# Products of constants on TensorE in the heads and tails of the attention stages, and a shorter entry and exit, in a four-level transformer kernel

## What is computed

```python
x = x + 0.5 * _L0_ffn_ref(_layernorm(x, axis=-1), ...)   # 8 experts, top 2
x = x + _L0_attn_ref(_layernorm(x, axis=-1), ...)        # 16 heads, softmax
x = x + 0.5 * _L0_ffn_ref(_layernorm(x, axis=-1), ...)
x = x + 0.5 * _L1_ffn_ref(_layernorm(x, axis=-1), theta, phi, theta_noise, phi_noise)
x = x + _L1_attn_ref(_layernorm(x, axis=-1), ...)        # a state that decays from token to token
x = x + 0.5 * _L1_ffn_ref(_layernorm(x, axis=-1), theta, phi, theta_noise, phi_noise)
...
# level 2: a stack of 6 windowed attention and ffn layers, attention, the stack again
# level 3: 8 experts top 2 (gated), attention with rotary angles and exp scores, 8 experts again
```

## Time and profile before

| what | us |
|---|---|
| three runs: lowest, median, highest | 5185.12, 5185.85, 5190.96 |
| the profiled execution | 5185.4 |
| its span in the trace (1.8 us lie outside it) | 5183.6 |
| entry: until the first load of stage 0 | 0 to 12.2 |
| angles in the entry: ten DVE operations | 4.21 to 7.78 |
| angles in the entry: ACT's table load, sine | 1.28, 0.42 |
| stage 0, experts of level 0 | 12.2 to 273 |
| ACT's idle time before L559 at 51.09 and in the next such place, 66.49 | 3.75, 3.71 |
| stage 1, attention of level 0 | 273 to 463 |
| one first_score (L927) at clock 0.50, at 1.00 | 1.67, 0.94 |
| stage 4, decaying attention of level 1 | 748 to 914 |
| stage 7, attention of level 2 | 2664 to 2887 |
| turn_negmax (L939) to turn_negmax in it, from the second on | 21.6 |
| one exponential of ACT in it | 1.02 |
| stage 10, attention of level 3 | 4797 to 4993 |
| last DVE operation, last DMA, end | 5176.94, 5178.12, 5183.6 |

### The profile page before, as it was taken

One profiled execution on the slowest core, in us unless ns is written; L12 is line 12 of the kernel. 1 busy time (PEld: TensorE's weight loads), 2 busy tenths in 40 slices (PEclk: granted clock), 3 DMA queues, 4 the chain that ended last, 5 costly groups with the idle time before them and its releaser, 6 DMA issues. The chain is left out here.

```text
span 5183.6 us, 141391 instructions
## 1 busy us (share of the span) xinstructions
PE 4899.3 (95%) x49076; PEld 3434.4 (66%) x49076; DVE 3885.8 (75%) x7068; ACT 3436.2 (66%) x5889; POOL 2889.7 (56%) x3477
## 2 busy tenths in 40 slices
PE   8989978699999999999979699999999999989899
PEld 5666656377777777777656377777777777656656
DVE  3274347589999999999856499999999999855655
ACT  3344333488888888888856378888888888852642
POOL 0010015588888888888720488888888888710200
PEclk9998988799999999999979799999999999989999
DMA  1000000112111112111100112121211111110000
GB/s 45 1 6 35 1 8 3 44 42 61 49 51 51 53 53 57 47 54 50 45 16 1 41 45 57 47 55 49 57 53 51 51 53 53 43 38 1 8 25 9
DMA packets 110453, 195.58 MB, mean 38 GB/s; under 512 B 21408, under 2 KB 28848, under 8 KB 110256
## 3 DMA queue, kind: packets, MB, share of 16 engines
q1 hardware_dynamic: 110256, 192.89, 13.3%
HBM read 53.36 MB, written 1.05 MB: 10 GB/s over the span
## 5 line engine op out<-in xcount | busy, mean ns | idle before, releaser
L3222 POOL TENSOR_TENSOR stage_qk<-stage_halves 128x1024 f32<-128x1024 f32 x384 | 908.7, 2366 | 16.6 <-DVE stage_halves L3380 1.6
L3258 POOL TENSOR_TENSOR stage_qk<-stage_qk,stage_rnorm 128x1024 f32<-128x1024 f32 x384 | 731.2, 1904 | 8.0
L3251 POOL TENSOR_TENSOR stage_probs<-stage_probs,stage_rsum 128x768 f32<-128x768 f32 x384 | 565.6, 1473 | 257.8 <-DVE stage_rsum L3409 257.8
L2973 ACT ACTIVATE stage_probsT<-stage_flip 96x512 f32<-96x512 f32 x768 | 452.8, 590 | 221.4 <-PE stage_flip L2610 220.8
L3377 DVE TENSOR_TENSOR stage_halves<-stage_wide,stage_tables 128x1024 f32<-128x1024 f32 x384 | 469.3, 1222 | 144.5 <-ACT stage_square L2927 98.0
L3380 DVE TENSOR_TENSOR stage_halves<-stage_wide,stage_tables 128x512 f32<-128x512 f32 x768 | 490.6, 680 | 0.0
L2927 ACT ACTIVATE stage_square<-stage_wide 128x1024 f32<-128x1024 f32 x384 | 393.5, 1025 | 141.1 <-PE stage_wide L2558 136.7
L3389 DVE TENSOR_REDUCE stage_norm<-stage_square 128x16 f32<-128x1024 f32 x384 | 463.7, 1208 | 29.1 <-issue 29.0
L2575 PE MATMUL stage_turn<-ident,stage_qk 128*128 128x128 f32 x3072 | 478.9, 279 | 6.5 <-ACT stage_qkT L2947 6.5
L2610 PE MATMUL stage_flip<-ident,stage_probs 128*96 128x128 f32 x3072 | 469.6, 275 | 8.1 <-POOL stage_probs L3251 6.9
L2624 PE MATMUL stage_pv<-stage_probsT,stage_v_win 96*64 96x64 f32 x12288 | 464.7, 226 | 2.6 <-ACT stage_ctxT L2980 1.5
(11 more groups left out here) (304 smaller groups left out, 9984.3 us busy)
## 6 DMA issues: line engine op xcount, KB each, us to landing
stage_v_win<-stage_v SPq DMA_DIRECT2D x384, 192.0 KB, 2.5
stage_v_win<-stage_v SPq DMA_DIRECT2D x384, 128.0 KB, 2.4
stage_v_win<-stage_v SPq DMA_DIRECT2D x192, 64.0 KB, 2.2
stage_wq<-in_T_wq SPq DMA_DIRECT2D x12, 512.0 KB, 4.2
stage_wk<-in_T_wk SPq DMA_DIRECT2D x12, 512.0 KB, 4.8
stage_wv<-in_T_wv SPq DMA_DIRECT2D x12, 512.0 KB, 3.4
stage_wo<-in_T_wo SPq DMA_DIRECT2D x12, 512.0 KB, 3.4
stage_w_up<-in_L_w_up SPq DMA_DIRECT2D x8, 512.0 KB, 6.6
```

The lines of the kernel that those rows point to most:

```text
L2973: nc.scalar.activation(probsT[:, n % 2].rearrange("p h t q -> p (h t) q"), tiles4(flip)[0:REACH], ACT.Copy)\
L3222: nc.gpsimd.tensor_tensor(qk[:, n, :], halves[:, n % 2, 0, :], halves[:, n % 2, 1, :], ALU.add)\
L3251: nc.gpsimd.tensor_tensor(probs[:, m % 2], probs[:, m % 2], rsum[:, m % 2].to_broadcast([P, 2, 2 * HALVES, REACH]), ALU.mult)\
L3258: nc.gpsimd.tensor_tensor(heads, heads, rnorm[:, n, :].rearrange("p (h o) -> p h o", o=1).to_broadcast([P, LH, LD]), ALU.mult).then_inc(at ...
```

## The change

Four parts.

**Entry.** The signals are raised by POOL, DVE, ACT and PE, a quarter each, and POOL sets `minus_half` first. SP loads the first two pieces of x and `ident` (signal `entered`, for which it waits) and then the other six pieces of x (signal `rest`). The work on the angles moves into the class `Angles` and stage 0: its four loads are issued after the experts' loads, DVE's chain stands after `statistics(1)` and ahead of `base(0)`, ACT's sine after `copy_xT(1)`.

```diff
+            if angles:
+                angles.load(sp)
+            if out is not None:
+                rows = out.rearrange("b (h p) d -> p (b h) d", p=P)
+                for step in range(steps):
+                    sp.wait_ge(*sig("x", step, 1))
+                    sp.dma_start(rows[:, step * T:(step + 1) * T, :], chip.x[:, step * T:(step + 1) * T, :]).then_inc(loaded["left"], 16)
+                sp.wait_ge(*loaded("left", 1))
...
                     if e == 3:
                         ahead(step, copy_xT)
+                        if angles and step == 0:
+                            angles.sines(act)
...
             route(0, chain)
+            if angles:
+                dve.wait_ge(*loaded("rest", 1))
             ahead(0, statistics)
+            if angles:
+                angles.reduce(dve)
```

```diff
+            def fill(count):
+                for n in range(count):
+                    nc.tensor.matmul(quad[:, n % GROUPS, 0:P], chip.ident[:, :], chip.ident[:, :], start=True, stop=True, skip_group_check=True)
+
+            def warm(count):
+                for n in range(count):
+                    nc.tensor.matmul(duo[:, n % 2, 0:P], chip.ident[:, :], chip.ident[:, :], start=True, stop=True, skip_group_check=True)
...
                 ins.then_inc(sig["negmaxT"], 1)
+                if step == B - 1:
+                    fill(6)
...
                 ins.then_inc(sig["scores"], 1)
+                if softmax and step == B - 1:
+                    fill(1)
...
                     if runs(s):
                         bank_free(("probs", s, 6))
                         score(s, 6)
+                    elif s == -2:
+                        warm(1)
...
+            warm(6)
             for s in range(-3, B + 3):
                 body(s)
```

```diff
                 ins.then_inc(sig["ynT_psum"], 1)
-                fill(FILL_Y)
+                if step < B - 1:
+                    fill(FILL_Y)
...
                     weigh(s - 3)
+                elif 1 <= s < 3:
+                    fill(5)
...
                     project_td(s - 1)
+                elif s == B + 1:
+                    fill_wide(1)
...
                     project_gv(s - 1)
+                elif s == B + 1:
+                    fill_wide(2)
...
                     project_kr(s - 1)
+                elif s == B + 1:
+                    fill_wide(3)
...
                     project_w(s - 1)
+                elif s == B + 1:
+                    fill_wide(1)
...
                     output(s - 4)
+                elif 1 <= s < 4:
+                    fill(2)
...
                     project_miu(s)
+                elif B + 1 <= s < B + 3:
+                    fill_wide(4 * (s - B))
...
                     turn_y(s - 3)
+                elif s < 3:
+                    fill(6)
```

253 lines of the change are left out of this document (202 added, 51 removed).

## The result

The changed kernel took 5160.03 us in the median of five runs (5149.42 to 5164.99), the kernel before 5185.85. The ratio is 0.9945, with a 95% interval from 0.9931 to 0.9959: 25.8 us less, clear of the 0.2% that can be told. The profiled execution took 5160.11, its span is 5158.3. The forecast was 5158, with a range from 5143 to 5177. The sum is right within 2 us, but several of its terms are off by 4 to 9 us and cancel, so that closeness is luck; most of this part is about that.

The account below looks back on a forecast made before the run. TensorE was taken to run at its upper clock except in short stretches where stages begin or end, 143 us of them at 1.2 GHz in the four touched stages. The terms sum to -27.7 us from 5185.85, giving 5158, range 5143 to 5177.

Parts of the forecast that it names:

- Start: Kernel entry: four engines share raising the signals, so stage 0 begins near 5.7 instead of 12.2: -6.5 us.
- Angles: Stage 0: the angles' work on DVE and ACT fits into idle gaps: 0; 3.0 us if the cover were gone.
- output: Kernel exit: three quarters leave before the last x is done, SP waits only for the last 256 KB: -3.2 us.
- Price of a product: Added products on PE: 0.46 us each at the low clock, 0.29 at the high one, free where PE waits anyhow.
- Decaying stage: Stage 4: products lift the clock; head -5 us (-8 to +4), tail -3 us (-5 to +2).
- First attention: Stage 1: products lift the clock; head -1 us (-4 to +2.5), tail -2.5 us (-4.4 to +4).
- Third attention: Stage 7: products lift the clock; head -3 us (-9 to +3.5), tail -4 us (-9 to +5).
- Fourth attention: Stage 10, head: seventeen products in one row ahead of the second turn nearly offset the clock's gain: +0.5 us (-3 to +6).
- Stages in between: Stages other than the four with added products, ends aside: no change, 0.
- A: Rival: the clock gives nothing net, only start and end count, -9.7 us, 5176; chance 0.12.
- C: Rival: the clock comes up nearly at once everywhere, -50.9 us, 5135; chance 0.13.
- B: Rival: products are paid at the low clock ahead of real work, +31.8 us, 5218; chance 0.04.

Follow-up runs that it names:

- e5_no_rwkv: The changed kernel with the decaying stage as in the kernel before (4 and 6 products, on the weights): 5178.73 us, ratio 0.9982.
- e1_ends: The changed kernel with its new start and exit, but all products of constants as in the kernel before: 5176.69 us, ratio 0.9978.
- e3_again: The changed kernel measured again without any edit, for a second profile: 5164.20 us, ratio 0.9955.
- e4_no_l3: The changed kernel without the 26 products at the head of stage 10 (attention of level 3): 5154.96 us, ratio 0.9946.
- e6_table: The changed kernel with one added exponential on ACT in the entry, so that its table is loaded there: 5158.94 us, ratio 0.9954.
- e9_all: The changed kernel with the early table load, products among the first scores of stages 1 and 7, 13 in stage 7's waits and 6 stand-ins: 5162.16 us.
- e11_l0_scores: The changed kernel with two more products ahead of each of the first five scores of step 0 in stage 1: 5171.68 us, ratio 0.9962.
- e12_burst: The changed kernel with 16 products in a row ahead of step 2's projection in stages 1 and 7: 5171.88 us, ratio 0.9969.

## Why the prediction was right, and where it was not

**Start, -6.5.** 6.07 came. The step of this term that failed is the one on ACT's tables: it was noted that a load at the start goes away, and not that the load left over would stand behind PE's first result. It costs 1.28 us, so the start is worth 4.8.

**Angles, 0, and output, -3.2.** Both as worked out: DVE had 2.61 us left and ACT 2.05, and 3.2 us went at the exit. Of the sum's 9.7 for the ends, the trace has 8.0; the run with them alone has 10.0, with a scatter of 12 us.

**Price of a product.** 0.46 low holds. The 0.29 at the high clock was too much, as it came from a short row of four; rows of fifteen and seventeen take 3.62 and 3.96 us. PE in the changed kernel, around the long rows:

```profile
754.42 3.62 PE L1957 MATMUL stage_inner<-ident 128*128 128x128 f32 x30
757.97 0.65 PE L1994 MATMUL stage_turn<-stage_mixd,stage_pack 128*64 128x256 f32 x2
...
884.02 1.95 PE L1962 MATMUL stage_wide<-ident 128*128 128x128 f32 x16
887.44 0.41 PE L2063 MATMUL stage_turn<-ident,stage_yn 128*128 128x128 f32 x2 [1.47 <-DVE stage_yn L2448]
889.06 0.78 PE L2071 MATMUL stage_turn<-stage_pack,stage_gated 128*128 128x128 f32 x4 [1.21 <-DVE stage_gated L2456]
...
4788.38 3.96 PE L973 MATMUL stage_duo<-ident 128*128 128x128 f32 x34
```

With two instructions for each product, these rows are 15, 8 and 17 products: 0.24, 0.24 and 0.23 each. The seventeen ahead of the second turn of stage 10 delay it from 11.6 to 13.1 us after the stage's start, 1.5 where 2.7 was forecast, and the third turn is already 0.5 us earlier than before. The last turn_y of stage 4 waits 1.47 us for DVE behind its eight products, so they were covered, as the term had it.

**Decaying stage, -8.** Right mechanism, both terms too small. project_td follows the fifteen products at once and comes 1.1 us earlier in the stage than before, where it waited 1.76 us for POOL. The second project_td is 0.3 us later than before, so up to there the products cost what they gave; the third is 4.6 us ahead and the fourth 6.8, which is where the low stretch of 782 to 795 and a short one behind it are gone. By the fifth of the eight turns of y the stage is still 6.8 us ahead (term: -5), and the tail gives 7.0 more (term: -3). The tail's term left out the clock's fall at 873.7, which the windows of the earlier trace rows did not cover. Some 3 to 5 of the 13.8 us may not be the products', as the two kernels without the new ones (e5_no_rwkv, e1_ends) took 160.5 and 162.4 in one trace each, where the kernel before took 165.5.

**First attention, -3.5.** -5.7 in this trace, but +2.5 to +5.4 in four of nine. Over the nine the stage takes 188.3 us in the mean, 1.7 less than before.

**Third attention, -7.** This is the term of the sum that failed. It held in two of six traces (-8.3), and in four the stage lost 2.1 to 2.8. Of its two parts, the tail (-4) came out at -5.2 in the first trace. The head (-3, from -9 to +3.5) did not: the first turn of the maxima is 2.8 us earlier, but the second is 4.2 us later and the fourth 7.3 us later than before. In two of the others (e3_again, e4_no_l3) the head gained its 2.8 us, and it was the tail that failed: its last turn of the maxima came 5.4 us later after the one before than it used to. What the sum lacked in both is a fall of the clock at a place where it had stayed up before; both terms only counted low stretches that were there already. For the head it comes behind the last product. PE's timeline of the changed kernel:

```profile
2664.06 0.71 PE L973 MATMUL stage_duo<-ident 128*128 128x128 f32 x4
2666.54 1.15 PE L963 MATMUL stage_quad<-stage_k_heads,stage_q_heads 32*128 32x256 f32 x16 [1.76 <-DVE stage_negmax L1722]
2667.61 1.02 PE L937 MATMUL stage_turn<-stage_pack,stage_xT 128*128 128x128 f32 x4
2670.43 0.69 PE L980 MATMUL stage_turn<-ident,stage_negmax 128*128 128x128 f32 x2 [1.79 <-DVE stage_v L1683]
2671.04 2.09 PE L963 MATMUL stage_quad<-stage_k_heads,stage_q_heads 32*128 32x256 f32 x16
```

The last two products end at 2664.8. Then PE waits 1.76 us, does a narrow score, waits 1.79, and the score at 2671.04 takes 2.09 us instead of 1.15. The clock fell behind the products, and it stayed down for 44 us: the second turn of the maxima came at 62.9 us instead of 58.7. The fall alone does not make the bad course. In the two good traces (e5_no_rwkv, e6_table) the clock falls at the same place, 25.9 us after the stage's start against 25.7 here, but is back at 46.4 us instead of 70.1. Among the operations that ran meanwhile are scores, but also turns, projections and `weigh`, so why it stayed down is not shown. The prediction had put the head's worst case at +3.5 us and taken it for the case in which products don't raise the clock. In fact they do, and a fall comes after them.

**Fourth attention, +0.5.** -3.8 in seven of eleven traces with these products, -2.6 in one, and +0.9, +3.4 and +4.1 in the others. The clock was up in one piece from 4788 to 4930. 2.8 of the 3.8 us were won behind the last turn of x, where no product stands and which no term counted. A low stretch there became shorter, from 10 to 3 us. Windows before and after:

```profile
4949.00:4959.00 10.00, 9.37 (x62) 5.86 (x66) 2.99 (x5) 4.08 (x4) 0.00 (x0) 0.51 0.01 2
4931.00:4934.00 3.00, 3.00 (x25) 2.08 (x24) 1.01 (x1) 0.81 (x1) 0.00 (x0) 0.50 0.00 0
```

**Stages in between, 0.** Stages 0 (less its table load), 2, 3, 5, 6, 8 and 9 together took 3.9 us more. They scatter by 1 to 5 us between traces of the same code, so this is no effect of the change that could be shown.

**Rivals and the total.** The sum came out since stages 4 and 10 gave 10 us more than forecast and stage 7 and the table 10 less. That is luck. Of the rivals, A (no net gain of the clock) is what the products of stages 7 and 10 come to over many executions: without either group the kernel took 5159.5 and 5155.0. C was the closest in stage 4 alone (counted its way from the earlier trace rows, that stage gains about 11 us; 13.8 were measured). B, products paid at the low clock in the way of real work, was small in the changed kernel's first trace (among the new ones in the tails, two products of stage 7, inside 2849 to 2855); it showed more in the runs that added some (e9_all, e11_l0_scores, e12_burst).

The best supported account is this. Of the 26 us, 8 to 10 are the two ends. The products in the decaying stage are worth 9 to 14 us by the traces of that stage, and 14.5 to 18.7 by the medians with and without them. By subtraction the 101 products in the three other stages give at most about 9 us, and e5_no_rwkv against e1_ends, the one pair of runs that has them alone as its difference, shows nothing for them (0.9982 and 0.9978). No version tried is clearly faster than the changed kernel.

What stays open: which condition decides between the good and the bad course of a stage, in its head and in its tail. It differs between executions of the same program, so something outside the program's order has a part in it. That the work is narrow (scores of 32 rows) was the theory of several runs; none of them isolates it, and e3_again, e9_all and e12_burst have products over all 128 rows inside stretches that stayed low.

## What to carry to other kernels

In this kernel, products meant to keep TensorE's clock up paid in the decaying stage, where rows of ten and fifteen of them stand in the head and the clock stayed up from 7 to 130 us after the stage's start. Put mostly one by one into empty slots, in stage 7, they left the clock to fall at a later place, and in four of six traces that cost more than it gave: PE was then slow for 17 to 44 us although 86 to 100% busy. So look for the place where the clock falls next, and take several traces, since one may show the good course and the next the bad. It also helps to add the doubtful part alone to the kernel before, besides taking it out of the whole: here that showed nothing for the 101 products, where subtraction had left them up to 9 us. And when an engine's first operation changes, look which table load or other first cost moves behind its first wait.
